# Four-layer graph network on one NeuronCore: another order of the opening, the last node tile normalised by VectorE, and 14 turns of the unit matrix on TensorE ahead of the first product

## The reference, cut to what matters

```python
edge_index = jnp.stack([src, dst])                       # 6144 edges
h = jnp.maximum(_layernorm(x, axis=-1), 0.0)
x = x + attention(h, edge_index, edge_type_5, ...)       # 16 heads, six 1024x1024 projections, mask from edges
h = jnp.maximum(_layernorm(x, axis=-1), 0.0)
x = x + relational(h, edge_index, edge_type_8, ...)      # 8 relations, root, gate
h = jnp.maximum(_layernorm(x, axis=-1), 0.0)
x = x + sage(h, src, dst, ...)                           # two layers
h = jnp.maximum(_layernorm(x, axis=-1), 0.0)
x = x + h @ W.T + bias3                                  # W: sparse, 1024x1024, entries in the first 384 rows and columns
```

## Time and profile before

| what | value |
| --- | --- |
| median of 3 runs | 928.15 us (927.82 to 928.22) |
| the profiled execution, its own time | 927.87 us |
| its span, first to last instruction | 926.1 us |
| TensorE busy | 98% of the span |
| VectorE busy | 66% |
| ScalarE busy | 39% |
| GpSimd busy | 53% |
| mean granted TensorE clock | 0.996 |

### The profile page before, as it was taken

How to read it: one execution, slowest core, us unless ns; L and a number is a source line. 1 busy time by engine, 2 the same in 40 slices (tenths; PEclk the granted TensorE clock), 3 DMA queues, 4 the chain that set the end, 5 groups by cost and what they waited for, 6 DMA issues and landing times.

```text
span 926.1 us, 13755 instructions
## 1 busy us (share of the span) xinstructions
PE 906.8 (98%) x4787; PEld 799.0 (86%) x4787; DVE 611.5 (66%) x993; ACT 359.2 (39%) x558; POOL 492.3 (53%) x436
## 2 busy tenths in 40 slices
PE   4999999999999999999999999999999999999998
PEld 4999999998888888888888888888888878888886
DVE  6998888896996735665656565565656565434545
ACT  6433333345885343223223223232325235224422
POOL 5334446775765515757657575756686402220463
PEclk8999999999999999999999999999999999999999
DMA  8998756634336644344554444444333534323412
GB/s 207 241 277 224 229 155 151 167 85 119 53 52 204 178 155 146 92 151 114 152 152 130 153 113 150 113 148 111 97 91 137 182 98 154 114 93 91 140 42 91
DMA packets 89907, 128.60 MB, mean 139 GB/s; under 512 B 34480, under 2 KB 67456, under 8 KB 89856
## 3 DMA queue, kind: packets, MB, share of 16 engines
q1 hardware_dynamic: 72784, 123.54, 43.8%
q0 software_dynamic: 15552, 0.11, 4.0%
q10 hardware_dynamic: 1520, 4.30, 1.4%
HBM read 117.17 MB, written 7.59 MB: 135 GB/s over the span
## 4 chain that ended last, share of the span: by engine, by line
PE 90%; DVE 3%; ACT 2%; POOL 1%; DMA 1%; issue 1%; POOLq 0%; DVEq 0%; ACTq 0%
PE ps L682 49%; PE ps L476 17%; PE ps L756 9%; PE ps L520 4%; PE ps L645 4%; PE ps L600 2%; PE ps L543 2%; PE ps L556 2%; DMA weight_d<-weight_sum,cell 1%; PE ps L435 1%; POOL weight_d L1890 1%; PE ps L892 1%; DVE wlo_all L1388 1%; POOL mean_lo L1869 0%; PE ps L443 0%
## 5 line engine op out<-in xcount | busy, mean ns | idle before, releaser
L1388 DVE TENSOR_TENSOR wlo_all<-raw,whi_all 128x1024 fp32r<-128x1024 f32 x120 | 200.4, 1681 | 119.6 <-ACT whi_all L972 118.5
L476 PE MATMUL ps<-acts,whi_all 128*128 128x384 f32 (+1 forms) x640 | 164.1, 337 | 0.8 <-DVE acts L1400 0.6
L1869 POOL TENSOR_TENSOR mean_lo<-mean_f,mean_hi 128x384 fp32r<-128x384 f32 x76 | 88.3, 1162 | 120.4 <-ACT mean_hi L1124 120.4
L1124 ACT ACTIVATE mean_hi<-mean_f 128x384 fp32r<-128x384 f32 x76 | 39.9, 525 | 277.2 <-DVE mean_f L1562 277.2
L682 PE MATMUL ps<-whi_all,mean_hi 128*128 128x512 f32 x452 | 139.5, 390 | 0.3 <-POOL mean_lo L1869 0.3
L682 PE MATMUL ps<-wlo_all,mean_hi 128*128 128x512 f32 x452 | 139.3, 389 | 0.0
L682 PE MATMUL ps<-whi_all,mean_lo 128*128 128x512 f32 x452 | 139.3, 389 | 0.0
L972 ACT ACTIVATE whi_all<-raw 128x1024 fp32r<-128x1024 f32 x120 | 125.1, 1050 | 32.0 <-PE ps L682 28.5
L476 PEld LDWEIGHTS ps<-acts,whi_all 128*128 128x128 f32 x640 | 116.8, 190 | 1.2 <-DVE acts L1400 0.9
L1890 POOL DMA_INDIRECT weight_d<-weight_sum,cell x48 | 95.5, 1989 | 30.4 <-DMA weight_d<-weight_sum,cell 17.5
L476 PE MATMUL ps<-acts,wlo_all 128*128 128x384 f32 (+1 forms) x320 | 107.6, 336 | 0.0
(11 more groups left out here) (211 smaller groups left out, 1705.6 us busy)
## 6 DMA issues: line engine op xcount, KB each, us to landing
raw<-in_L_gnn_weight SPq DMA_DIRECT2D x64, 512.0 KB
rows_b<-rows_d SPq DMA_DIRECT2D x24, 384.0 KB, 4.8
raw<-in_L_gnn_w_gate SPq DMA_DIRECT2D x16, 512.0 KB
raw<-in_L_gnn_W_self SPq DMA_DIRECT2D x16, 512.0 KB
raw<-in_L_gnn_W_neigh SPq DMA_DIRECT2D x16, 512.0 KB
count_d<-total_r SPq DMA_DIRECT2D x8, 576.0 KB
rel_r<-count_d SPq DMA_DIRECT2D x8, 576.0 KB, 4.5
raw<-in_L_gnn_wq SPq DMA_DIRECT2D x32, 128.0 KB
```

The source lines that it names most:

```text
L476: mm = pe.matmul(ps[:, j % 2, 0:N], stationary[j % RING][:, k, :], acts[:, a, moving, k, :], start=i == 0, stop=i == 3 * KT - 1)
L1124: act.activation(mean_of(q, k, 0)[:, 0, :], sums_of(q, k), ACT.Copy).then_inc(S["mean_hi"], 1)
L1388: dve.tensor_tensor(wlo_row[slot], raw[slot][:, :], whi_row[slot].bitcast(F32), ALU.subtract)\
L1869: pool.tensor_tensor(mean_of(q, k, 1)[:, 0, :], sums_of(q, k), mean_of(q, k, 0)[:, 0, :].bitcast(F32), ALU.subtract).then_inc(S["mean_lo"], 1)
```

## The change

- SyncE loads the first node tile in two halves with semaphores of their own.
- VectorE: the statistics of the three tiles are interleaved with the shifts in another order. The two edge keys (`edge_keys`) come right after the first tile's statistics, the type row and relation key (`edge_types`) only after the low part of the first node tile. The third node tile is normalised by VectorE (`start_norm`, no ReLU; the ReLU is applied by ScalarE's copy and by a max in the low part), where ScalarE did it before. The copy to `e_col` and the three first softplus instructions come after all the low parts.
- TensorE: the edge rows are turned after all of h, into bank 2. Eight turns of the unit matrix stand ahead of them and six behind, 14 in all (`stay_busy`), whose result nobody reads. The first product no longer waits for `edge_cols`.
- ScalarE: the third tile's two normalising instructions go; its root is taken before `start_high(0)`.
- GpSimd issues the six bias transfers before its constants instead of after them.
- At the end, the third node tile is normalised by VectorE (384 features) instead of ScalarE, in the same manner.

```diff
-            for nt in range(NT):
+            sp_.dma_start(xres[:, 0, 0:HALF], x_rows[:, 0, 0:HALF]).then_inc(x_half, 16)
+            sp_.dma_start(xres[:, 0, HALF:D], x_rows[:, 0, HALF:D]).then_inc(x_part[0], 16)
+            for nt in range(1, NT):
                 sp_.dma_start(xres[:, nt, :], x_rows[:, nt, :]).then_inc(x_part[nt], 16)
...
             for n, (nt, k0, k1) in enumerate(START):
-                if n == 2:
-                    turn_edges()
                 pe.wait_ge(S["h_ready"], n + 1)
...
+            def stay_busy(n):
+
+                for _ in range(n):
+                    pe.transpose(ps[:, 0, 0:P], ident[:, :], ident[:, :])
+
+            stay_busy(8)
+            pe.wait_ge(S["start_lo"], 1)
+            turn_edges()
             pe.wait_ge(S["bcol_in"], 16 * 6)
-            pe.wait_ge(S["start_lo"], 1)
+            stay_busy(6)
             pe.transpose(ps[:, 2, 0:6 * KT], b_in[:, :], ident[0:6 * KT, 0:6 * KT]).then_inc(S["bcol_made"], 1)
-            pe.wait_ge(S["edge_cols"], 1)
...
             norm_relu_0(*START[1])
+            norm_std(0, 2)
             start_high(0)
-            norm_std(0, 2)
-            norm_relu_0(*START[2])
-            norm_relu_0(*START[3])
             tile_high(0, 0)
...
             norm_std(3, 2)
-            norm_relu(3, 2, h, FIRST_THIRD)
-            tile_turned_high(Y_H3 + 2, 2, NT)
+            tile_turned_high(Y_H3 + 2, 2, NT, ACT.Relu)
...
+            dve.wait_ge(x_half, 16)
+            half_stats(0, 0)
+            dve.wait_ge(x_part[0], 16)
+            half_stats(0, 1)
+            var_of(0, 0)
+            edge_keys()
+            dve.wait_ge(x_part[1], 16)
+            half_stats(1, 0)
+            norm_shift(0, 0)
+            half_stats(1, 1)
+            var_of(0, 1)
+            dve.wait_ge(x_part[2], 16)
+            half_stats(2, 0)
+            norm_shift(0, 1)
+            half_stats(2, 1)
+            var_of(0, 2)
...
             dve.wait_ge(S["h_ready"], 1)
             turn_tile(0, 0)
+            norm_shift(0, 2)
+            start_norm(*START[2])
+            start_norm(*START[3])
             start_low(0)
-            dve.wait_ge(S["edges_turned"], 1)
-            dve.tensor_copy(e_col[:, :, :], ps[:, 0, 0:4 * EC].rearrange("p (f c) -> p f c", f=4))\
-               .then_inc(S["edge_cols"], 1)
+            edge_types()
             start_low(1)
             start_low(2)
             start_low(3)
+            dve.wait_ge(S["edges_turned"], 1)
+            dve.wait_ge(S["bcol_made"], 1)
+            dve.tensor_copy(e_col[:, :, :], ps[:, 2, P:P + 4 * EC].rearrange("p (f c) -> p f c", f=4))\
+               .then_inc(S["edge_cols"], 1)
+            dve.wait_ge(S["etw_in"], 16)
+            link(dve.tensor_scalar(sp[:, 0, :], etw_b[:, :], 0.0, None, ALU.max))
+            link(dve.tensor_scalar(sp[:, 1, :], etw_b[:, :], -1.0, None, ALU.mult))
+            dve.tensor_tensor(sp[:, 2, :], etw_b[:, :], sp[:, 1, :], ALU.max).then_inc(S["sp_max"], 1)
...
-            tile_turned_low(Y_H3 + 2, 2, NT)
+            dve.wait_ge(S["shift_ready"], NT * 4)
+            dve.tensor_scalar(h[:, NT - 1, 0:N], xres[:, NT - 1, 0:N], rstd[:, NT - 1, :], shift[:, NT - 1, :],
+                              ALU.mult, ALU.add).then_inc(S["h_ready"], 1)
```

More of the change, by code:

```diff
@@ L1277, in norm_shift @@
                    .then_inc(S["shift_ready"], 1)
-            def start_stats(nt):
-                dve.wait_ge(x_part[nt], 16)
-                norm_stats(0, nt)
-            for nt in range(NT):
-                start_stats(nt)
-                if nt < NT - 1:
-                    norm_shift(0, nt)
-            dve.wait_ge(S["edges_in"], 16 * 4)
-            dve.scalar_tensor_tensor(e_row[:, KEY, :], e_in[:, 0, :], float(N), e_in[:, 1, :], ALU.mult, ALU.add)\
-               .then_inc(S["key_made"], 1)
@@ L1299, in _, with edge_keys @@
-            link(dve.tensor_scalar(sp[:, 1, :], etw_b[:, :], -1.0, None, ALU.mult))
-            dve.tensor_tensor(sp[:, 2, :], etw_b[:, :], sp[:, 1, :], ALU.max).then_inc(S["sp_max"], 1)
+            def edge_keys():
+                dve.wait_ge(S["ends_in"], 16 * 2)
+                dve.scalar_tensor_tensor(e_row[:, KEY, :], e_in[:, 0, :], float(N), e_in[:, 1, :], ALU.mult, ALU.add)\
+                   .then_inc(S["key_made"], 1)
+                dve.scalar_tensor_tensor(e_row[:, KEY_T, :], e_in[:, 1, :], float(N), e_in[:, 0, :], ALU.mult, ALU.add)
```

62 lines of the change are left out of this document (39 added, 23 removed).

## The result

The changed kernel took **933.72 us** in the median of 6 runs (931.90 to 937.92), the kernel before 927.88 (927.80 to 928.22): ratio 1.0066, 95% interval 1.0053 to 1.0080. Forecast were 929.1 us, range 927.1 to 930.6, with 0.18 for slower. The profiled execution of the change took 933.22 us with a span of 931.4, which is 5.3 us more than the 926.1 of before.

What follows compares the result with a forecast made beforehand. VectorE's list up to L1400, not TensorE, was taken to bound the opening. Opening +1.0 and end -0.1 made +0.9 us on the median of 928.15: 929.1 us, range 927.1 to 930.6.

Steps and rivals of the forecast that it cites:

- What bounds the opening: Opening: VectorE's list up to L1400 sets its end; 10.58 us from the second weight tile's turn to 28.57 stay unchanged.
- Lands ... at 8.4 us: Opening, loads: the last of x's three transfers, issued at 1.7 us, lands 6.7 us later, at 8.4 us.
- I take its data as landed by then: Opening, VectorE: the first weight tile's data is there when VectorE reaches its turn at 10.2 us.
- my +1.0: Opening: forecast loss of 1.0 us, with bounds of -0.7 and +1.4.
- The stop behind GpSimd: Opening, VectorE: the relation key, reached at 14.2 us, waits until 15.5 for GpSimd's 2.36 us low part.
- They cost nothing: Opening, TensorE: the first eight unit-matrix turns run from about 13.6 to 15.3 us, before the edge rows at 15.8.
- rival 4: Opening: VectorE early, turns at low clock; copy to `e_col` waits for bias rows; 928.5 us, chance 0.10.
- The high clock is worth nothing: Opening, TensorE: a faster clock gains nothing, since the third output tile waits for VectorE anyway (0.57 us before).
- rival 3: Ahead of the third output tile: TensorE idles 2.7 us, the clock falls, costing 1.8 us; 930.9 us, chance 0.13.
- The end: Last node tile: VectorE normalises in 0.45 us, not stopped by GpSimd; -0.1 us, at best -0.2.
- rival 2: End: VectorE's normalising waits for GpSimd until 919.66, TensorE turns 0.3 us later; 929.5 us, chance 0.22.

Runs made afterwards that it cites:

- the mask edit alone: The kernel before with four more of the mask's 48 scatters on GpSimd put ahead of the counts': 928.07 us, ratio 0.9989.

## Why the prediction was wrong

- **What bounds the opening: right.** "The opening's gain or loss is the shift of that one start": 3.69 in, 3.69 out. Between lie 10.57 to 10.59 us in every kernel that left this stretch alone but one: with the mask edit alone TensorE came later than VectorE, and it was 11.08.
- **"Lands ... at 8.4 us" and "I take its data as landed by then": the step that failed.** The landing of x's third tile was taken from before, and that of the first weight tile from no row, though SyncE's list was changed (its first weight transfer was issued at 2.66 us instead of 2.19). They came at 10.03 and 12.88 us. The turn of the first weight tile, forecast at 10.2, started 2.7 us late, and all later steps carried it: the second's started at 21.68 where 18.9 was forecast. Undone alone, the split gives back 2.3 us of the turn's start, and the split alone costs before 2.5. The change's first line had no term in my sum. The assumption on the weight tile fails without the split too: in the four kernels with x whole and the rest of the order VectorE waited 0.94 to 1.46 us for it and turned it at 11.03 to 11.94 us.
- **The miss in numbers.** Measured minus forecast is 4.6 us. The opening took 2.7 us more than my +1.0, the fall of the clock 1.5, the end 0.3: 4.5 together.
- **The stop behind GpSimd: right in kind, a little short in size.** Expected was a row of over 1 us ending with L1839; it was the cast that ended with it, 1.28 us instead of 0.21. The pair was held 1.1 us, where I had 1.3. I had looked at the key only, which has two inputs in SBUF. The Trainium skill (SBUF — State Buffer, Who interferes with whom) names the cast as well among the operations that can take the shared ports, and by that sentence the row stopped would have been the first of the pair, as it was. Two smaller terms: the normalising instructions took 1.00 us together, where I took 1.2, and a softplus row beside GpSimd's `moved` rows took 0.28 us instead of 0.17, the 0.1 that I took.
- **"They cost nothing": wrong.** A turn followed the next by 0.24 and later by 0.21 us, about as said; but h's last turns waited for VectorE's normalising until 15.05, so the eight ran from 16.8 and the six to 20.5. The copy to `e_col` waited 0.50 us, and 1.36 us once the stop was gone. This was rival 4's mechanism. I had given it 0.10, and only as an alternative to the stop; both happened, one behind the other.
- **The high clock is worth nothing: right** for this order, shown by the turns alone. (By the granted clock, do not tell a low from a high clock: its column reads 1.00 at 8 and at 12.5 us. Only the turns' duration, 0.42 and 0.27 us, does.)
- **The fall ahead of the third tile: rival 3, given 0.13.** Its place and price were right (2.36 us of waiting against 2.7, 1.5 us against 1.8), its chance was not. The forecast itself implied the wait: the first product at about 17.6 and the third tile at 29.5 were both in the text. In the profiles the clock fell behind waits for an output tile of 1.84, 2.23, 2.33, 2.34, 2.36 and 2.37 us, and stayed behind others of 2.36 (bias transfers back) and 1.56 (turns alone): with a wait near 2 us I should have given it even odds or better.
- **The end: rival 2.** 0.92 us beside GpSimd, TensorE's turn 0.23 later instead of 0.1 earlier. The Trainium skill's rule on `tensor_scalar` (SBUF — State Buffer, Who interferes with whom) was the better guide; the low parts, by which I argued against it, read PSUM.

## What to carry to other kernels

A landing time belongs to the set of transfers it was measured with: split one of them, and every landing behind it is unknown until a trace shows it. Give each line of a diff a term in the sum, above all the transfer that looks harmless. Work that only raises the clock pays only where TensorE is the next bound; elsewhere it makes a longer gap, and the gap may cost the clock.

## What the runs showed of the hardware that was not expected

- Two transfers of 256 KB in place of one of 512 KB, ahead of two more of 512 KB, lowered the rate in the stretch from 4 to 5 us to 162 to 261 GB/s in the seven kernels with a split; the thirteen with the whole tile have 382 to 419. VectorE began x's second tile anywhere from 7.13 to 9.73 us, before at 6.51. The Trainium skill (Perfetto Trace Analysis, DMA Optimizations) says that splitting may let the whole complete sooner where the DMA engines are generally idle. Here they were not (share 1.01 from 4 to 5 us before); the half came 0.6 us sooner (3.60 against 4.20 us) and the third tile some 2 us later. Why is open.
- A cast, int32 to fp32 on 48 partitions, stands behind a GpSimd instruction with two SBUF inputs (1.28 us instead of 0.21), as a `tensor_scalar` in fp32 does (0.92 instead of some 0.4).
- With turns alone ahead of the first product the products followed each other by 0.17 us from the first on, where before they took 0.32 until 21.6 us. The Trainium skill (TensorE: Matmul & The Clock Gate, Part 4) has transposes not count as busy in the same way; these runs do not bear that out.
- The granted clock of the trace is no witness ahead of its first fall: with the end alone and no turns it reads 1.00 from 14 to 22 us, though the products follow each other by 0.32 us there.
- Some one in eight runs of the kernel before (15 of 119) is 4 to 6 us longer. In the kernel with turns alone such a run is the program's own doing: the mask's last scatters end a round later. For the kernel before this is likely, not shown.
